# Batch 1 of the shared expert: the last 128 inputs of eight blocks computed from whole-number weights

## What is computed

```python
def dequant_gptq(qweight, scales, zeros, groupsize):      # groupsize = 128
    q = qweight[k // PACK, :] >> (k % PACK * 4)[:, None] & 15
    z = zeros[:, n // PACK] >> (n % PACK * 4)[None, :] & 15
    s = scales.astype(jnp.float32)
    zp = (z.astype(jnp.float32) + 1.0) * s
    return q.astype(jnp.float32) * s[k // groupsize] - zp[k // groupsize]
gate = x2 @ Wg            # x2: tokens x 512, Wg and Wu: 512 x 1376
up = x2 @ Wu
inter = gate * jax.nn.sigmoid(gate) * up
out = (inter @ Wd).astype(jnp.float16)
...
x = x + _layernorm(_L0_attn_ref(_layernorm(x, ...), ...))   # state-space layer
x = x + _layernorm(_L0_ffn_ref(_layernorm(x, ...), ...))    # the 4-bit layer
x = x + _layernorm(_L1_attn_ref(_layernorm(x, ...), ...))   # attention
x = x + _layernorm(_L1_ffn_ref(_layernorm(x, ...), ...))    # mixture of experts
```

## Time and profile before

| | us |
|---|---|
| median of three runs | 802.54 (802.38 to 802.8) |
| the profiled execution | 807.23 |
| its span | 805.3 |
| PE busy in the span | 683.3 (85%) |
| DVE busy | 684.8 (85%) |
| ACT busy | 470.1 (58%) |
| POOL busy | 481.6 (60%) |

### The profile page before, as it was taken

The page is one execution under the profiler, slowest core; times in us unless marked ns, Lnnn a source line. Parts: engine busy times, 40 slices in busy tenths (PEclk is TensorE's granted clock), DMA queues, the critical chain, the costliest instruction groups (busy, mean ns, idle before and its releaser), DMA issues. The chain is left out here.

```text
span 805.3 us, 8451 instructions
## 1 busy us (share of the span) xinstructions
PE 683.3 (85%) x2794; PEld 323.7 (40%) x2794; DVE 684.8 (85%) x697; ACT 470.1 (58%) x805; POOL 481.6 (60%) x252
## 2 busy tenths in 40 slices
PE   7979889987776888555546879999999999999995
PEld 6623333322121332111111324444445456887885
DVE  6869999999999999999999998998274565585778
ACT  5468787895755675867664547757325347323333
POOL 2419999999999999999999970220002014341130
PEclk9989989999878999558857999999999999999998
DMA  8434133334502715630334309962040030000011
GB/s 261 94 92 151 43 115 104 131 130 141 206 24 87 244 60 170 229 131 27 104 131 160 121 1 284 265 190 64 0 157 1 1 105 0 1 1 1 0 53 52
DMA packets 42358, 83.19 MB, mean 103 GB/s; under 512 B 6825, under 2 KB 10340, under 8 KB 42060
## 3 DMA queue, kind: packets, MB, share of 16 engines
q1 hardware_dynamic: 42316, 82.67, 32.1%
HBM read 71.44 MB, written 11.21 MB: 103 GB/s over the span
## 5 line engine op out<-in xcount | busy, mean ns | idle before, releaser
L2403 POOL TENSOR_TENSOR dbu<-rep_du,bc 128x1024 f32<-128x1024 f32 x127 | 296.8, 2365 | 2.2 <-DMA bc<-bc_scratch 1.0
L1895 ACT ACTIVATE psum<-rep_dt,aneg 128x512 f32<-128x512 f32 x256 | 166.1, 682 | 116.9 <-DVE hc L1245 94.3
L1234 DVE TENSOR_TENSOR_SCAN psum<-psum,dbu 128x1024 f32<-128x1024 f32 x89 | 203.3, 2285 | 3.4 <-POOL dbu L2403 1.6
L985 PE MATMUL psum<-hc,stk 128*32 128x512 f32 x512 | 83.4, 728 | 60.5 <-POOL hc L2412 41.6
L1245 DVE TENSOR_TENSOR hc<-psum,bc 128x1024 f32<-128x1024 f32 x89 | 108.9, 1224 | 3.1
L2412 POOL TENSOR_TENSOR hc<-hc,bc 128x1024 f32<-128x1024 f32 x39 | 92.1, 2362 | 6.1 <-DVE hc L1234 6.0
L1234 DVE TENSOR_TENSOR_SCAN hc<-psum,dbu 128x1024 f32<-128x1024 f32 x39 | 88.9, 2280 | 1.6 <-ACT psum L1895 0.9
L719 PE MATMUL psum<-xf_hi,gu_lo 128*128 128x512 f16 x176 | 67.5, 383 | 0.0
L719 PE MATMUL psum<-xf_hi,gu_hi 128*128 128x512 f16 x176 | 67.4, 383 | 0.1
L719 PE MATMUL psum<-xf_lo,gu_hi 128*128 128x512 f16 x176 | 67.3, 383 | 0.0
L719 PE MATMUL psum<-xT,w_g 128*128 128x512 f32 x120 | 59.7, 647 | 2.6 <-ACT rep_du L2040 2.6
(11 more groups left out here) (301 smaller groups left out, 1444.3 us busy)
## 6 DMA issues: line engine op xcount, KB each, us to landing
rep_dt<-rep_scratch SPq DMA_DIRECT2D x60, 256.0 KB, 3.4
rep_du<-rep_scratch SPq DMA_DIRECT2D x60, 256.0 KB, 4.3
cw<-c_scratch SPq DMA_DIRECT2D x11, 768.0 KB, 8.2
qw<-qgu_in SPq DMA_DIRECT2D x11, 512.0 KB, 6.4
bc<-bc_scratch SPq DMA_DIRECT2D x16, 256.0 KB, 4.6
rep_scratch<-du_t SPq DMA_DIRECT2D x14, 256.0 KB, 2.0
rep_scratch<-dt_t SPq DMA_DIRECT2D x14, 256.0 KB, 2.3
qw<-qd_in SPq DMA_DIRECT2D x11, 256.0 KB, 6.8
```

Source lines behind the costliest of these rows:

```text
L985: last = pe.matmul(y_rows(k), stk[:], hc[:, (i + k // 2) % HCS, k % 2, :], start=False, stop=(s == GN - 1))
L1234: dve.tensor_tensor_scan(h, a, dbu[:, i % DBS].rearrange("p e t -> p (e t)"), 0.0, ALU.mult, ALU.add)\
L1895: last = act.activation(psum[:, 2 * (i % 2) + e, :], rep_dt[:, cc % 2, k, :], ACT.Exp, scale=aneg[:, k, c, n:n + 1])
L2403: pool.tensor_tensor(dbu[:, i % DBS], rep_du[:, cc % 2, k:k + 2, :], bc[:, n, :].unsqueeze(1).broadcast_to([P, 2, L]), ALU.mult).then_inc( ...
```

## The change

For blocks 1 to 4 and 6 to 9 of batch 1 (`GROUPED`), the last 128 of the 512 inputs are taken out of the gate and the up product, which then have 9 matmuls each. Their part is made from the whole numbers q - z - 1, which float16 holds exactly, so that it needs two matmuls (`group_part`: whole numbers x high half, whole numbers x low half of the input) into bank 4. ACT multiplies that bank by the scale of each output (`group_scaled`), into `sg` for the gate and into `it` for the up product. DVE adds the gate bank to `sg` (`gate_sum`), ACT takes silu of `sg` in place (`ffn_silu_sum`), DVE adds the up bank to `it` (`up_sum`) and multiplies the two (`times_sum`). The cast and the low half follow as before.

The whole numbers of the eight blocks are copied inside the on-chip memory by DMA while batch 0 runs (`keep_ints`), each before its staging slot is loaded again. The scales are read with one output per partition by two DMAs (`group16`) and cast to float32 on DVE. Several steps change place too: the two reductions for the attention weights now stand ahead of block 0 of batch 1; the pieces of `between` for i = 0, 1, 3 and 4 stand ahead of the low half; the second and third residual sums stand together at block 1; and on ACT `group_scaled` of the next block's gate stands ahead of the cast.

```diff
+GROUPED = (1, 2, 3, 4, 6, 7, 8, 9)
...
+        ints = {i: at(f"ints{i}", 35 + n / 2, [2 * P], F16) for n, i in enumerate(GROUPED)}
+        group16 = at("group16", 206.625, [2, IC], F16)
+        group32 = at("group32", 206.75, [2, IC])
...
+            def keep_ints(i):
+                if i not in GROUPED:
+                    return
+                sp_.wait_ge(q16_used, i + 1)
+                sp_.dma_start(ints[i][:], cw[i % SLOTS][:, 0, 2 * (KH - 1) * P:2 * KH * P]).then_inc(ints_kept, 16)
+            def kept_up_to(i):
+                return sum(j <= i for j in GROUPED)
             def stage_again(i):
+                if i > SLOTS:
+                    sp_.wait_ge(ints_kept, 16 * kept_up_to(i - SLOTS))
                 sp_.wait_ge(wlo_gu, i - SLOTS + 1)
                 sp_.wait_ge(wlo_d, i - SLOTS + 1)
                 stage(i)
             wait_work(sp_, ("out", 1, NT - 1))
             stage(3)
+            keep_ints(1)
             for i in range(SLOTS, IC):
                 stage_again(i)
+                if i > SLOTS:
+                    keep_ints(i - SLOTS + 1)
+            sp_.wait_ge(ints_kept, 16 * kept_up_to(IC - SLOTS))
+            keep_ints(IC - 3)
             sp_.wait_ge(wlo_gu, 8)
             sp_.wait_ge(wlo_d, 8)
             load(wqraw[:].rearrange("p a b c -> p (a b c)"), wq_in, ld_att)
@@ -678,9 +707,15 @@
             load(moe_w["gate"][0][:], gate_in.rearrange("p (c k) -> p c k", c=KH), ld_att)
             load(gam[:], gamma_in.broadcast_to([P, H]), ld_att)
             load(bet[:], beta_in.broadcast_to([P, H]), ld_att)
+            keep_ints(IC - 2)
+            for j in range(2):
+                sp_.dma_start(group16[:, j, :], sgu_in[2 * (KH - 1) + j:2 * KH - 1 + j, :]
+                              .rearrange("r (i n) -> n (r i)", n=P),
+                              allow_slow_non_contiguous=True).then_inc(ld_group, 16)
             sp_.wait_ge(wq_done, 2)
             sp_.wait_ge(wr_stored, 16 * KH)
             load(moe_w["wr"][0][:], wr_dram.rearrange("(k p) n -> p k n", p=P), ld_moe[0])
+            sp_.wait_ge(ints_kept, 16 * len(GROUPED))
...
+                def group_part(i, j):
+                    n = 2 * GROUPED.index(i) + j
+                    if n:
+                        pe.wait_ge(group_done, n)
+                    else:
+                        pe.wait_ge(ints_kept, 16 * len(GROUPED))
+                    w = ints[i][:, j * P:(j + 1) * P]
+                    pe.matmul(psum[:, Y_BANK, :], w, xf_hi[1][:, KH - 1, :], start=True, stop=False)
+                    pe.matmul(psum[:, Y_BANK, :], w, xf_lo[1][:, KH - 1, :], start=False, stop=True)\
+                        .then_inc(group_ready, 1)
...
                 for i in range(IC):
                     k = b * IC + i
+                    grouped = b == 1 and i in GROUPED
...
@@ -1023,11 +1071,15 @@
                         item = (name, b, i)
                         start(item)
                         parts = []
-                        for kk in range(KH):
+                        for kk in range(KH - 1 if grouped else KH):
                             w = slice((2 * kk + j) * P, (2 * kk + j + 1) * P)
                             parts += halves(gu_hi[:, i, w], gu_lo[:, i, w], xf_hi[b][:, kk, :],
                                             xf_lo[b][:, kk, :])
+                        if grouped and j == 0:
+                            group_part(i, 0)
                         product(item, parts).then_inc(work_ready, 1)
+                        if grouped and j == 1:
+                            group_part(i, 1)
...
+            def gate_sum(i):
+                k = IC + i
+                item = ("g", 1, i)
+                wait_work(dve, item)
+                dve.wait_ge(group_done, 2 * GROUPED.index(i) + 1)
+                dve.tensor_tensor(sg[:, k % 2, :], bank(item), sg[:, k % 2, :], ALU.add).then_inc(taken_sem(item), 1)
+            def up_sum(i):
+                k = IC + i
+                item = ("u", 1, i)
+                wait_work(dve, item)
+                dve.wait_ge(group_done, 2 * GROUPED.index(i) + 2)
+                dve.tensor_tensor(it[:, k % 2, :], bank(item), it[:, k % 2, :], ALU.add).then_inc(taken_sem(item), 1)
+            def times_sum(i):
+                k = IC + i
+                dve.wait_ge(silu_done, GROUPED.index(i) + 1)
+                wait_taken(dve, ("u", 1, i))
+                dve.tensor_tensor(it[:, k % 2, :], sg[:, k % 2, :], it[:, k % 2, :], ALU.mult).then_inc(it_done, 1)
...
                 k_b = qkv[:, :, DH:2 * DH].unsqueeze(2).broadcast_to(full)
                 link(dve.tensor_tensor(sc[:], q_b, k_b, ALU.mult))
                 link(dve.tensor_reduce(smax[:], sc[:], AX.X, ALU.max))
+                if b == 0:
+                    gate_sum(6)
                 dve.tensor_tensor(sc[:], sc[:], smax[:].unsqueeze(3).broadcast_to(full), ALU.subtract)\
...
                 link(dve.tensor_tensor(sc[:], pr[:], v_b, ALU.mult))
                 dve.tensor_reduce(num[:], sc[:], AX.X, ALU.add)
+                if b == 0:
+                    gate_sum(7)
                 link(dve.reciprocal(den[:], den[:]))
                 link(dve.tensor_tensor(num[:], num[:], den[:], ALU.mult))
...
@@ -1533,11 +1609,16 @@
                 if i == 0:
                     ffn_stats16(b)
                 if i == 1:
-                    ffn_inv16(b)
-                    ffn_add16(b, 0)
-                    ffn_add16(b, 1)
+                    if b == 0:
+                        ffn_add16(b, 1)
+                        ffn_add16(b, 2)
+                    else:
+                        ffn_inv16(b)
+                        ffn_add16(b, 0)
+                        ffn_add16(b, 1)
                 if i == 2:
-                    ffn_add16(b, 2)
+                    if b:
+                        ffn_add16(b, 2)
                     ffn_add16(b, 3)
                     stats(("att", b), x_tiles(b))
...
+            dve.wait_ge(ld_att, 16 * 7)
+            dve.tensor_reduce(wqkv[:, :, 0:DH], wqraw[:], AX.X, ALU.add).then_inc(wq_done, 1)
+            dve.tensor_reduce(bqkv[:, 0:DH], bqraw[:], AX.X, ALU.add).then_inc(wq_done, 1)
+            dve.wait_ge(ld_group, 32)
+            dve.tensor_copy(group32[:], group16[:]).then_inc(group_set, 1)
             for i in range(IC):
+                if i in GROUPED and i not in (6, 7, 8):
+                    gate_sum(i)
                 if i == IC - 1:
                     low_moe(0, [2, 3])
-                ffn_times(1, i)
+                if i in GROUPED:
+                    up_sum(i)
+                    if i == 1:
+                        ffn_inv16(0)
+                        ffn_add16(0, 0)
+                    times_sum(i)
+                else:
+                    ffn_times(1, i)
                 if i == 9:
                     norm_tile("moe", 0, 2, xnc)
                     norm_tile("moe", 0, 3, xnc)
+                if i in (0, 1, 3, 4):
+                    between(0, i)
                 ffn_low(1, i)
-                if i == 0:
-                    dve.wait_ge(ld_att, 16 * 7)
-                    dve.tensor_reduce(wqkv[:, :, 0:DH], wqraw[:], AX.X, ALU.add).then_inc(wq_done, 1)
-                    dve.tensor_reduce(bqkv[:, 0:DH], bqraw[:], AX.X, ALU.add).then_inc(wq_done, 1)
-                if i < 8:
+                if i in (2, 5, 6, 7):
                     between(0, i)
                 if i == 7:
+                    gate_sum(8)
                     between(0, 8)
                 if i == 8:
...
+            def group_scaled(i, j):
+                k = IC + i
+                if i == 1:
+                    act.wait_ge(group_set, 1)
+                act.wait_ge(group_ready, 2 * GROUPED.index(i) + j + 1)
+                if j:
+                    act.wait_ge(itlo_done, k - 1)
+                act.activation((it if j else sg)[:, k % 2, :], psum[:, Y_BANK, :], ACT.Identity,
+                               scale=group32[:, j, i:i + 1]).then_inc(group_done, 1)
+            def ffn_silu_sum(i):
+                k = IC + i
+                wait_taken(act, ("g", 1, i))
+                act.activation(sg[:, k % 2, :], sg[:, k % 2, :], ACT.Silu).then_inc(silu_done, 1)
             def ffn_high(k):
                 b, i = divmod(k, IC)
-                wait_taken(act, ("u", b, i))
+                if b == 1 and i in GROUPED:
+                    act.wait_ge(it_done, GROUPED.index(i) + 1)
+                else:
+                    wait_taken(act, ("u", b, i))
...
             for k in range(NB * IC):
                 b, i = divmod(k, IC)
-                ffn_silu(k)
+                if b == 1 and i in GROUPED:
+                    if i - 1 not in (0, 2, 5, 6, 8):
+                        group_scaled(i, 1)
+                    ffn_silu_sum(i)
+                else:
+                    ffn_silu(k)
...
                 if b == 1 and i == 10:
                     high_moe(0, [2, 3])
+                if b == 1 and i + 1 in GROUPED and i != 5:
```

(19 more changed lines are left out.)

## The result

| | before | after |
|---|---|---|
| median (lowest to highest), 13 runs each, us | 804.20 (802.38 to 807.81) | 806.54 (804.81 to 811.75) |
| profiled execution / its span, us | 807.23 / 805.3 | 810.21 / 808.3 |

The changed kernel takes 1.0038 times as long, 95% interval 1.0024 to 1.0053, which is 1.9 to 4.3 us. It is slower, as forecast, and by about the size forecast (+2.2). The time itself, 806.54 us, is 1.7 us above the forecast of 804.8 and outside its range of 803.2 to 805.8.

A forecast was written before the change was run, and what follows sets the result against it. PE was taken to bound batch 1: 16 matmuls less save 3.45 us, but waits for low halves (blocks 1, 7, 8) and late tiles (block 9) leave +2.2 us; added to 802.54, this gave 804.8 us, range 803.2 to 805.8.

The forecast's parts named there:

- D: How much later (+) or earlier (-) a down product starts than in the kernel before, in us.
- Block 1: PE waits 1.1 us for the low half; the down product starts at 594.9 instead of 594.68, D = +0.2.
- Blocks 2 to 5: Low halves come in time, ACT's new order costs nothing; D falls 0.43 us per block, to -0.75 at block 3.
- Block 6: ACT's exponential stands behind the up part's scaling (done 632.5), yet PE does not wait; D = -1.6 for down product 6.
- Block 7: PE waits for bank 4 and the low half, 1.8 us together; down product at 648.2, D = -0.2.
- Block 8: The low half stands behind attention sums and statistics on DVE; PE waits 2.3 us, down product at 657.9, D = +1.75.
- Block 9 and the end: Last turned tiles start at 664.2 and 664.85 instead of 662.20; PE goes on 2.2 us later, with no slack afterwards.
- Before batch 1: Loads wait for copies in batch 0 at no cost; block 8's load is closest, with at least 1.5 us left.
- 1: Rival: the low halves of blocks 1, 7 and 8 come early enough, waits stay covered; about 799.8 us, chance 0.20.
- 2: Rival: gain and waits cancel, block 9's tiles or half of block 8's wait being covered; 802.5 us, chance 0.13.
- 3: Rival: the scales' two DMAs land late for block 0's multiplication, 9 us at worst; 808 to 814 us, chance 0.07.
- 4: Rival: the clock falls to half in PE's new gaps, costing 1.7 us; +3.9, 806.4 us, chance 0.10.

The follow-up runs named there:

- e6: The changed kernel with ACT's cast of each block ahead of the scaling of the next block's gate part; 807.13 us, 1.0042 of before.
- e1: Kernel before plus only what lies ahead of batch 1 (copies, scales, cast, moved reductions), nothing on whole numbers; 804.74 us, 1.0014 of before.
- e10: The changed kernel with its eight copies made by POOL in place of DMA; 807.12 us, 1.0042 of before.
- e4: The changed kernel with only blocks 6 to 9 on whole numbers, blocks 0 to 5 in the order of before; 808.91 us, 1.0058 of before.
- e8: The changed kernel with blocks 2 to 5 on whole numbers instead, low halves first as before; 805.06 us, 1.0019 of before.
- e12: e8 with POOL's copies and, on DVE, the third residual sum ahead of low half 2, norms ahead of low halves 3 and 4; 803.28 us, 0.9986 of before.
- e13: Kernel before with only e12's order on DVE, nothing on whole numbers, no copies; 803.25 us, 0.9992 of before.
- e5: The changed kernel with block 8's up sum, product and low half ahead of the attention's statistics on DVE; 805.51 us, 1.0018 of before.
- e2: Kernel before with only the changed kernel's order on DVE, nothing on whole numbers, no copies; 803.49 us, 0.9994 of before.

## Why the prediction was wrong, step by step

The mechanism and the difference came out as forecast. The absolute time did not: 804.8 us with a range of 803.2 to 805.8 was forecast, and 806.54 was measured (inside the wider range of 800.4 to 807.2, which leaves 0.1 out on each side). The step that failed is the last one of the sum, "the runs shown have their median 4.7 us lower, at 802.54, and I add the same". That base was too low: thirteen runs of before have their median at 804.20, which is 1.66 of the 1.74 us. The three runs known then are the three lowest of the thirteen; they span 0.4 us, the thirteen 5.4. The range had room for longer scalings and shorter hand-overs and none for the base; set out from 804.20, the same sum gives 806.4 and 804.9 to 807.5. Why those three were low stays open.

For the difference, +2.2 was forecast. The stretch has +2.43, the medians +2.3, the ratio +3.1 (1.9 to 4.3), which is 0.6 us more than the stretch gives, within its interval. For the profiled execution 809.4 was forecast and 810.21 measured; 0.59 of the 0.8 us lie ahead of the stretch. One thing in the agreement is luck: both profiles have the clock's fall A. Had only one of them had it, the same two kernels would have shown +0.75 or +4.1 in the stretch.

Times of after less the 0.59 us of its later start.

- **PE loses 16 matmuls.** Right: down product 2 follows 1 at 602.88 - 595.54 = 7.34, which is 7.77 less two steps of 0.216.
- **Block 0.** I had PE wait 0.3; it did not: D = -0.33 in place of -0.1. Without weight, since block 1 waits.
- **Block 1.** Low half at 594.20 (594.2), PE waits 1.24 (1.1) and starts at 594.95 (594.9).
- **Blocks 2 to 5.** Covered, down product 3 at 609.63 (609.6). The timeline has it at 610.20 before, where the chain of the earlier trace rows that I used has 610.36, so D is -0.57 and not -0.75. e6 confirms the order on ACT.
- **Block 6.** Exponential at 632.46 (632.5), low half at 636.92 (637.05). D = -1.44 for down product 6 (-1.6).
- **Block 7.** Low half at 647.28 (647.5); PE waits 0.36 for bank 4 and 0.98 for the low half, 1.3 where I had 1.8; down product at 648.03 (648.2). D = -0.19 (-0.2).
- **Block 8.** Low half at 657.08 (657.15), wait 2.29 (2.3), down product at 657.82 (657.9). D = +1.83 (+1.75).
- **Block 9 and the end.** Last turned tiles at 664.25 (664.2). Here is the one term of the end that was mis-sized: PE went on at 665.51, not 665.3. I had given the last tile 0.43 us, and from the start of the pair it took 1.26 (with `x8`, 1.25). End of the layer 673.28 (673.05): +2.43 in place of +2.2.
- **Before batch 1.** No cost in the profile of after, as forecast. But the cover was thinner than I had it: block 8's load has its last DMA at 524.97 and landed 9.0 us later, 0.7 us ahead of its unpacking at 534.65 (times of that profile as they stand), where I had at least 1.5. In e1 DVE waited 0.74 us at that place, and PE did not. Whether the copies cost time in other executions is not shown.
- **Rivals.** 1 and 2 did not occur. 3 is excluded by the landing of 5.3 us (3.4 to 6.6 in the other kernels), with other loads beside them: the DMA share was 0.89 to 1.12 from 550 to 556 us. The packets under 512 B rose from 6825 to 9801; in e10, which has the scales and no DMA copies, to 9673, that is by 2848 for 2816 elements. By the Trainium skill (DMA: Bandwidth & Descriptors, section Rules for kernel authors) each element is a descriptor of its own; the packets agree, and it did not bear on the time. 4 did not occur in the profile of after, but in e4 and e6, at 1.1 us where I had 1.7.

Beside the base, what failed was not a step of this sum but what I took from it afterwards: that blocks ahead of the attention weights keep their gain by themselves (e8).

## What to carry to other kernels

When work is moved from the bounding engine to idle ones, follow the chain of dependences instruction by instruction through each queue; the free time of an engine says nothing of it (DVE had 41% free and the kernel still lost 2.4 us). Take the exchange only where the chain has slack, and put the chain's own instructions ahead of the rest there: the same eight matmuls less cost 0.9 us in one order (e8 against e1) and gave 1.5 us in the other (e12 against e13). The size of the largest wait isn't what its removal brings; e5 took 2.3 us of waiting away and gained 0.6. And a forecast of an absolute time needs a range for its base too: three runs that agreed within 0.4 us were 1.7 us below the median of thirteen.

## What the runs showed of the hardware

Behind the attention weights' small matmuls the granted clock fell to half in five of the fourteen profiled executions, and stayed at 1.00 in nine. e1 and e2, whose PE instructions are the same there, are one of each: the 2.4 GHz level kept in e1, the 1.2 GHz level in e2. The fall is worth 1.7 us, as much as eight matmuls. In windows of 2 us of e1 and of e2 (PE, PEld, DVE, ACT, POOL, then the clock):

```profile
624.00:626.00 2.00, 2.00 (x12) 1.05 (x12) 1.58 (x2) 0.00 (x0) 0.00 (x0) 1.00 0.00 0
626.00:628.00 2.00, 2.00 (x11) 0.88 (x9) 1.94 (x2) 0.00 (x0) 0.00 (x0) 1.00 0.00 0
```

```profile
622.00:624.00 2.00, 2.00 (x8) 0.89 (x8) 1.58 (x2) 0.00 (x0) 0.00 (x0) 0.53 0.00 0
624.00:626.00 2.00, 2.00 (x8) 0.67 (x6) 1.94 (x2) 0.00 (x0) 0.00 (x0) 0.62 0.00 0
```

The same holds for PE's gap of 2.3 us at block 8: in e4 the clock behind it was 0.64 and 0.51, in after and e10 1.00 behind a gap of 2.29. Windows of e4 and of after:

```profile
656.00:658.00 2.00, 1.56 (x4) 0.57 (x5) 0.90 (x3) 1.81 (x4) 0.00 (x0) 0.64 0.52 203
658.00:660.00 2.00, 2.00 (x6) 0.76 (x5) 1.68 (x4) 1.97 (x3) 0.00 (x0) 0.51 0.02 6
```

```profile
658.00:660.00 2.00, 1.58 (x8) 0.76 (x9) 0.90 (x3) 1.96 (x4) 0.00 (x0) 1.00 0.56 214
```

What decides it is open. So one profile against another can differ by 1.7 us in one place without any change in the kernel, which is as much as was to be told here.
